# Causal small attention: the second-half products of probabilities and values three slots later in the round, and the pieces behind them one to seven slots later

## What is computed

```python
q = x @ Wq.T + bq
k = x @ Wk.T + bk
v = x @ Wv.T + bv
q = q.reshape(b, l, N, H).transpose(0, 2, 1, 3)
k = k.reshape(b, l, N, H).transpose(0, 2, 1, 3)
v = v.reshape(b, l, N, H).transpose(0, 2, 1, 3)
q = apply_rope(q) * scale
k = apply_rope(k)
dots = jnp.einsum('bnih,bnjh->bnij', q, k)
i = jnp.arange(l)
mask = i[:, None] < i[None, :]
dots = jnp.where(mask, jnp.float32(-100000.0), dots)
attn = jax.nn.softmax(dots, axis=-1)
o = jnp.einsum('bnij,bnjh->bnih', attn, v)
o = o.transpose(0, 2, 1, 3).reshape(b, l, d)
return o @ Wo.T + bo
```

## Time and profile before

| | us |
|---|---|
| median of three runs | 4948.01 |
| lowest and highest run | 4946.1, 4949.84 |
| span of the profiled execution | 4944.1 |
| twelve rounds of l1att in the middle of its stage | 247.13 |
| twelve rounds of gqa in the middle of its stage | 228.43 |
| TensorE busy over the span | 3835.4 |

### The profile page before, as it was taken

How to read it: one execution, slowest core, us unless ns; L and a number is a source line. 1 busy time by engine, 2 the same in 40 slices (tenths; PEclk the granted TensorE clock), 3 DMA queues, 4 the chain that set the end, 5 groups by cost and what they waited for, 6 DMA issues and landing times. The chain is left out here.

```text
span 4944.1 us, 90876 instructions
## 1 busy us (share of the span) xinstructions
PE 3835.4 (78%) x25840; PEld 2735.3 (55%) x25840; DVE 3465.1 (70%) x9524; ACT 2341.8 (47%) x5537; POOL 2386.9 (48%) x3900
## 2 busy tenths in 40 slices
PE   7889797779999799568869937567775887799365
PEld 5666565656666466456646626422332665466265
DVE  7887775666666676566658856669998664588566
ACT  3444464355666466234436624345553454366243
POOL 5666442534344442446643354367776662233453
PEclk9999898789999899679979959779998999899698
DMA  6000332100000232133323311212121330133113
GB/s 234 0 0 1 112 124 76 52 20 1 0 0 1 72 124 94 39 124 107 107 80 117 110 38 47 73 48 65 63 62 64 114 117 28 51 120 112 36 46 87
DMA packets 244547, 341.24 MB, mean 69 GB/s; under 512 B 26976, under 2 KB 187120, under 8 KB 243120
## 3 DMA queue, kind: packets, MB, share of 16 engines
q1 hardware_dynamic: 230960, 309.19, 18.8%
q0 software_dynamic: 13184, 27.22, 1.6%
HBM read 182.77 MB, written 147.26 MB: 67 GB/s over the span
## 5 line engine op out<-in xcount | busy, mean ns | idle before, releaser
L522 DVE TENSOR_REDUCE l0att_rowmax<-l0att_S 128x2 f32<-128x512 f32 x512 | 339.8, 687 | 125.2 <-PE l0att_S L701 122.9
L893 POOL TENSOR_TENSOR wb_prob<-wb_prob,wb_rden 128x128 f32<-128x128 f32 (+1 forms) x512 | 248.2, 506 | 360.7 <-DVE wb_rden L1070 360.3
L522 DVE TENSOR_REDUCE l1ffn_rowmax<-l1ffn_S 128x2 f32<-128x512 f32 x512 | 337.6, 686 | 87.2 <-PE l1ffn_S L701 83.1
L1983 POOL TENSOR_TENSOR ssm_hc<-core_AW_all,ssm_Cs 128x512 f32<-128x512 f32 x256 | 320.8, 1268 | 131.2 <-DVE core_AW_all L2129 98.1
L1434 POOL DMA_INDIRECT results<-e_y,e_back x220 | 213.7, 971 | 289.4 <-DVE e_y L1662 269.9
L935 ACT ACTIVATE wb_prob<-wb_biased,wb_nmax 128x128 f32<-128x128 f32 (+1 forms) x512 | 228.6, 447 | 236.0 <-DVE wb_nmax L1063 233.6
L2228 PE MATMUL ssm_Y<-ssm_hc,core_ident 128*128 128x512 f32 x512 | 287.8, 672 | 56.8 <-POOL ssm_hc L1983 31.1
L2129 DVE TENSOR_TENSOR_SCAN core_AW_all<-core_AW_all,ssm_U 128x512 f32<-128x512 f32 x256 | 310.6, 1213 | 1.0 <-ACT core_AW_all L2072 0.6
L701 PE MATMUL l1ffn_S<-l1ffn_K,l1ffn_Q 128*128 128x512 f32 x512 | 251.0, 494 | 75.1 <-DVE l1ffn_rowmax L522 42.3
L1775 PE MATMUL e_H<-e_xT,e_W1s 128*128 128x128 f32 x1760 | 252.0, 288 | 70.2 <-issue 50.6
L701 PE MATMUL l0att_S<-l0att_K,l0att_Q 128*128 128x512 f32 x512 | 248.6, 489 | 60.4 <-DMA l0att_K<-bounce 47.5
(11 more groups left out here) (498 smaller groups left out, 11511.3 us busy)
## 6 DMA issues: line engine op xcount, KB each, us to landing
bounce<-l0att_parts SPq DMA_DIRECT2D x128, 256.0 KB, 2.8
bounce<-l1ffn_parts SPq DMA_DIRECT2D x128, 256.0 KB, 2.8
ssm_Cs<-c_rows SPq DMA_DIRECT2D x128, 256.0 KB, 3.1
routed<-core_Y SPq DMA_DIRECT2D x8, 2048.0 KB, 24.8
l0att_Q<-bounce SPq DMA_DIRECT2D x128, 128.0 KB
l0att_K<-bounce SPq DMA_DIRECT2D x128, 128.0 KB
bounce<-l1att_parts SPq DMA_DIRECT2D x64, 256.0 KB, 2.8
l1ffn_Q<-bounce SPq DMA_DIRECT2D x128, 128.0 KB
```

Of the source, the lines that this page charges most:

```text
L522: dve.tensor_reduce(out=rowmax[:, jp, qt, 2 * pair:2 * pair + 2], in_=S[a % 2][:].rearrange("p (j k) -> p j k", j=2)[:, :, 0:keys(qt)], op ...
L893: ins = pool.tensor_tensor(out=prob[:, w_ % NP, a:b], in0=prob[:, w_ % NP, a:b], in1=rden[:, w_ % NP, n:n + 1].to_broadcast([P, b - a]), o ...
L1983: pool.tensor_tensor(out=hc[:, u % 4], in0=hs[:, u % 4], in1=Cs[:, n % 4], op=ALU.mult)\
```

## The change

In the stages with rotary embedding, the weigh of the second half moves from slots 1 and 2 to slots 4 and 5, and ACT's copy of O from slot 3 to slot 6. n0 moves from slot 5 to 8, n1 from 6 to 12, on from 12 to 13 and out from 14 to 15. `v` stays in slot 4, h in 7, qq in 9, kk in 10 and mt0 in 11. No computing instruction is added or removed, and the other small attention stages keep their order.

```diff
         if rope:
-            plan = {3: "mt1", 4: "v", 5: "n0", 6: "n1", 7: "h", 9: "qq", 10: "kk", 11: "mt0", 12: "on", 14: "out"}
+            plan = {3: "mt1", 4: "v", 7: "h", 8: "n0", 9: "qq", 10: "kk", 11: "mt0", 12: "n1", 13: "on", 15: "out"}
+            WEIGHS = ((1, 4), (0, 10))
         else:
             plan = {3: "mt1", 4: "v", 5: "n0", 6: "n1", 7: "h", 9: "qk", 10: "on", 11: "mt0", 13: "out"}
+            WEIGHS = ((1, 1), (0, 10))
...
-                for jp, at in ((1, 3), (0, 13)):
+                for jp, at in WEIGHS:
                     n = r - jp
-                    if u == at and inside(n):
+                    if u == at + 2 + (jp == 0) and inside(n):
                         act.wait_ge(weighed.sem, weighed.at(n, jp + 1))
...
-                    for jp, at in ((1, 1), (0, 10)):
+                    for jp, at in WEIGHS:
                         if u in (at, at + 1) and inside(r - jp):
                             weigh(r - jp, jp, u - at)
```

## The result

| | before | after |
|---|---|---|
| median of five runs each, us | 4946.8 | 4963.27 |
| lowest and highest run | 4942.66, 4949.84 | 4956.27, 4970.89 |
| time of the profiled run, and its span | span 4944.1 | 4956.27, span 4954.5 |

The ratio is 1.0038, with a 95% interval from 1.0027 to 1.005: the change makes the kernel slower. The two medians lie 16.5 us apart, which alone is a ratio of 1.0033. The profiled execution of after was the fastest of its five, so its span shows +10.4 us.

The account below looks back on a forecast made before the run. The prediction took the loop over DMA to bound the rounds: 4944.1 + 5.6 (gqa) - 9.5 (l1att) - 1.2 - 6 (ends) + 12.8 (clock) = 4945.8 for the span, 4949 us for the median, no change; range 4935 to 4963.

Parts of the forecast that it names:

- The third rival: In both stages the clock falls in 16 or more of 24 rounds, giving 4960 to 4971 us; chance 0.18.
- What bounds the kernel: Loop over DMA from slot 8 through part, stores and sends; rounds of 19.5 us in gqa, 19.8 in l1att.
- n0's 0.47 us in the loop: n0 between slot 8 and kk lengthens each round by 0.47 us; +5.6 us over gqa's twelve rounds.
- The mask wait: PE's wait at slot 1 for POOL's mask, 2.12 us in l1att and 1.4 in gqa, goes away.
- The new waits: PE waits about 0.5 us at slot 7, 0.6 at slot 13, and 1.5 to 1.7 at slot 8.
- I take nine of 24, four in gqa and five in l1att, nearer the row of 1.4: Clock falls behind the waits at slots 7 and 8, nine rounds at 1.42 us each: +12.8 us.
- I take -3 us a stage: The last three rounds of each stage, without part, gain 3 us, between 0 and 5; -6 us in all.
- The -1.2 ahead of l1att's twelve: The round ahead of l1att's twelve comes to the same loop bound from 20.9 us; -1.2 us, an estimate.
- The rule on short waits: Skill's rule: such short waits leave the clock alone, sum stays -11.1 us; the prediction let the trace decide instead.
- The landing did not move with PE: Rival: K's landing at slot 8 moves with PE, so PE's work sets the round; 4899 us, chance 0.05.
- the weigh stayed clear of the mask: Rival: mt1 and slot 4's weigh still wait for POOL, losing 0.5 to 1 us a round; chance 0.03.
- That the clock would hold: Rival: at most one clock fall in 24 rounds, so -11.1 us and 4937 us, faster; chance 0.14.

Follow-up runs that it names:

- a_fill8: The changed kernel with nine mask products of no use on PE at slot 8, ahead of its wait for K; 0.9987 of before.
- a_n0_late: The changed kernel with n0 at slot 12, n1 at 13, on at 14, out at 15, so n0 is behind kk; 0.9966 of before.
- a_pieces_only: The changed kernel with the weigh back in slots 1 and 2 and the copy in slot 3, only the pieces moved; 0.9994 of before.
- c_weigh11: The changed kernel with n0 at slot 12, n1 13, on 14, out 15, and the first half's weigh in slots 11 and 12; 0.9933 of before, 4910.84 us.
- a_v6: The changed kernel with the projection of v in slot 6, behind the weigh, instead of slot 4; 1.0066 of before.
- b_fill1: The kernel before with twelve mask products of no use on PE at slot 1, ahead of the wait for the mask; 0.9974 of before.
- a_n0_late_fill8: The changed kernel with n0 at slot 12, n1 13, on 14, out 15, and five mask products ahead of slot 8's wait; 0.9956 of before.
- c_in_loop: The changed kernel with n0 at slot 12, n1 13, on 14, out 15, and five mask products each at slots 8 and 9; 0.9984 of before.
- a_send_first: The changed kernel with SP issuing send(r+1, 1) ahead of store(r+2) in the two changed stages; 1.0213 of before.

## Why the prediction was wrong

The forecast was 4949 us and no change; it came out 4963.27 and slower, just past the end of the range. The third rival comes nearest: it asked for a fall in 16 or more of the 24 rounds, and there were 15, or 17 by length.

**What bounds the kernel** was read rightly. The round is set by the loop from slot 8 over kk and `part`, and then the stores and sends back to slot 8. The clock-whole rounds of after are 19.3 to 19.5 us in gqa, for a forecast of 19.5, and 19.4 to 20.1 in l1att, for 19.8; in `a_fill8`, where none falls, the twelve average 19.5 and 19.6. So l1att's loop was put 2 us too long (235.60 for 237.6). n0's 0.47 us in the loop was right too (`a_n0_late` -0.5, `a_pieces_only` 19.5), and so was slot 8 to `part`: 8.6 us for a forecast of 8.1 + 0.47.

**The mask wait** went, and nothing of it came back at mt1 but 0.3 us a round in l1att. **The new waits** were sized well: 0.6 for 0.5 at slot 7, 0.5 to 0.6 for 0.6 at slot 13, 1.7 for 1.5 at slot 8 in gqa. At slot 8 in l1att it is 1.2 us for a forecast of 1.7 (1.5 in its five rounds with the clock whole, 1.1 in the seven with a fall).

**The step that failed** is "I take nine of 24, four in gqa and five in l1att, nearer the row of 1.4", the +12.8 us of the sum. There were 15 rounds, and 17 falls by their length: nearer to before's l1att, where it was eight rounds of twelve (the prediction's "about nine" is right by length). Against `a_fill8`, where no round falls, the term measured 248.3 - 233.8 = 14.5 us in gqa for a forecast of 4 x 1.42 = 5.7, and 245.4 - 235.6 = 9.8 in l1att for 7.1, together 24.3 for 12.8. That the clock carries this loss is shown, for `a_fill8` gets it back by 9 products a round.

Why so many rounds fell is shown less well. The forecast took the price of the wait at slot 8 from the lone wait of 1.4 us at slot 1. But the 0.6 of slot 7 stands just ahead, as the prediction says itself. For the pair speaks `a_pieces_only`: its gqa has no wait at slot 7, and eleven rounds with 0.75 to 1.9 us at slot 8 kept the clock (it fell behind 2.5), while in after seven rounds of l1att fell with 0.8 to 1.4 us there and 0.6 ahead.

```profile
PE gqa_S L701 <- DMA gqa_K<-bounce: 14.0, 12, 2.5
```

These kernels differ in more than the wait of slot 7, though, and no run took that wait alone away at the same wait of slot 8. And the sum of the two doesn't decide a single round: it is 1.4 to 2.0 us in l1att's rounds that fell and 1.8 to 2.5 in those that held.

**A fall of twice the length** was not thought of, though the kernel before had one. Such a round is 2.9 to 3.1 us above 19.5 and not 1.42, as the two of 22.4 and 22.60 us show. 17 x 1.42 = 24.1 us stands against 24.3 measured, so the price of a fall held, and only the count was off.

**"I take -3 us a stage"** for the last rounds failed as well. They gained nothing: what lies behind l1att's twelve rounds is 0.6 us shorter, behind gqa's 2.2 us longer. The -1.2 ahead of l1att's twelve held (-1.3; -0.1 in gqa), so all these make +0.2 us against the -7.2 that -6 and -1.2 make. The mask wait fell away at r = 14 and came back at slot 8:

```profile
4124.76 0.28 PE L701 MATMUL gqa_S<-core_causal,core_ident 128*128 128x256 bf16 x1 [2.08 <-DMA gqa_K<-bounce]
```

In the sum, then, the loop gave +5.4 us for +5.6 in gqa and -11.5 for -9.5 in l1att, the clock +24.3 for +12.8, the ends +0.2 for -7.2: together +18.4 us for the two stages, where the medians of the whole kernel differ by 16.5. In the profiled executions it is +10.4, since the other stages, which the change doesn't touch, took 8.0 us less in that one. The miss is these two terms, the falls first and the ends second.

**The rule on short waits.** By what the prediction cites of the Trainium skill, page "TensorE: Matmul & The Clock Gate", section "Why this matters for your kernels", these short waits should leave the clock alone. The traces here don't agree: 15 of 24 rounds fell behind waits of 0.6 and 0.8 to 2.3 us, and in `a_fill8`, where the second wait is mostly filled, none did.

**The other rivals.** The landing did not move with PE; the weigh stayed clear of the mask. That the clock would hold was wrong for this kernel, but `a_fill8` shows what it would give: the prediction's 4937 against before's 4948 is 0.9978, and 0.9987 was measured.

## What to carry to other kernels

When a wait is taken away in front of an engine that a loop through a queue bounds, it reappears at the loop's own wait, and the clock has to be priced anew there. In these runs a pair of waits close together had falls in as many rounds as one long wait (15 of 24 each), so the short one ahead should not be left out; that the sum is the right measure is not shown. A piece of work is costed by where it lies on the loop: half a microsecond between the landing and the work that starts the next transfer costs its full length each round, the same piece behind that costs little or nothing. Taking work off that way brings its full length only until the next bound is met: `c_weigh11` got 0.6 us of 0.86. And where TensorE must wait, a few products of no use ahead of the wait can be cheaper than the wait itself, as long as the clock does fall there: in l1att of `a_n0_late` it did not, and five products cost 0.2 us a round.

## What the runs showed of the hardware

The clock can stay at half speed for 6.8 us in a round of 20 us in place of 3.4, and the slowed work then lengthens the loop that caused the wait. Whether it falls at a given wait can't be read from that wait's length alone: in after it held behind 0.6 and 1.9 us in one round of l1att (at 2386) and fell behind 0.6 and 1.0 in another (at 2262), and in gqa of `a_v6` it held behind 3.5 us and fell behind 2.3. What decides in a single round stays open; what the runs show is that a_fill8, b_fill1, a_n0_late_fill8 and c_in_loop, which fill the wait with products, had no fall in 96 rounds. (In b_fill1 that takes in gqa, which had none before either.) In `a_send_first`, PE's wait for a small DMA behind 1 MB of stores in the same queue ended six microseconds after its issue and was 2.7 to 3.1 us in each round.
